# The clearing of an edge layer's sums moved behind its first gathers, on one Trainium2 core

## The reference

```python
def _gine_layer(x, src, dst, edge_attr, eps, We, be, W1, b1, gamma, beta, W2, b2):
    e = edge_attr @ We + be
    m = jax.nn.relu(x[src] + e)
    agg = jax.ops.segment_sum(m, dst, num_segments=x.shape[0])
    h = ((1.0 + eps) * x + agg) @ W1 + b1
    mu = jnp.mean(h, axis=0)
    var = jnp.mean(jnp.square(h - mu), axis=0)
    h = (h - mu) * jax.lax.rsqrt(var + BN_EPS) * gamma + beta
    h = jax.nn.relu(h)
    return jax.nn.relu(h @ W2 + b2)
```

## Time and profile before

| | |
|---|---|
| median of 3 runs | 876.57 us (871.54 to 879.27) |
| the profiled execution | 878.66 us |
| its span, first to last instruction | 876.9 us |
| mean granted clock of PE | 0.965 of full speed |
| busy: PE, DVE, ACT, POOL | 90%, 80%, 62%, 32% of the span |
| an edge layer, from its first gather to its last sum | about 68 us, of which there are four |

### The profile page before, as it was taken

How to read it: one execution, slowest core, us unless ns; L and a number is a source line. 1 busy time by engine, 2 the same in 40 slices (tenths; PEclk the granted TensorE clock), 3 DMA queues, 4 the chain that set the end, 5 groups by cost and what they waited for, 6 DMA issues and landing times.

```text
span 876.9 us, 12030 instructions
## 1 busy us (share of the span) xinstructions
PE 786.6 (90%) x3566; PEld 601.8 (69%) x3566; DVE 697.3 (80%) x1253; ACT 543.0 (62%) x1034; POOL 283.1 (32%) x230
## 2 busy tenths in 40 slices
PE   2979899899889899979999999988999989999895
PEld 2667565477467668756777777776777867878674
DVE  7989856799966968886798878977889778997635
ACT  2288213566563423556797778877788677864656
POOL 3000387877300000016760067400863028610000
PEclk9989999799989999997999999999999999999998
DMA  5323246788472330417994199823996249942001
GB/s 117 103 80 107 69 131 195 227 248 243 150 261 85 118 131 1 154 39 178 215 223 120 35 222 222 206 92 84 225 221 161 86 126 215 220 105 65 32 6 54
DMA packets 61329, 122.12 MB, mean 139 GB/s; under 512 B 9096, under 2 KB 22698, under 8 KB 61269
## 3 DMA queue, kind: packets, MB, share of 16 engines
q0 software_dynamic: 22096, 52.18, 27.2%
q1 hardware_dynamic: 39173, 69.17, 25.1%
HBM read 105.60 MB, written 15.73 MB: 138 GB/s over the span
## 4 chain that ended last, share of the span: by engine, by line
PE 59%; DVE 21%; ACT 11%; DMA 6%; issue 3%; SPq 0%; ACTq 0%; DVEq 0%
PE ps L712 12%; PE ps L1043 9%; PE ps L1082 6%; PE ps L1026 6%; PE ps L1067 6%; DVE z_parts L1955 5%; PE ps L820 5%; DMA onehot_dst<-onehot_rows 4%; PE ps L965 3%; PE ps L911 3%; DVE gathered_parts L1702 2%; DVE w L1462 2%; PE ps L704 2%; ACT slot_recs L1146 2%; ACT queued L1298 2%
## 5 line engine op out<-in xcount | busy, mean ns | idle before, releaser
L680 POOL DMA_INDIRECT queued<-node_rows,srci x92 | 144.4, 1569 | 198.3 <-DMA node_rows<-work 152.1
L1043 PE MATMUL ps<-z_parts,onehot_dst 128*125 128x512 f32 x664 | 189.4, 397 | 2.9 <-DMA onehot_dst<-onehot_rows 2.6
L1955 DVE SCALAR_TENSOR_TENSOR z_parts<-ps,z_parts 128x512 fp32r<-128x512 f32 x216 | 146.0, 689 | 34.5 <-ACT z_parts L1354 30.0
L712 PE MATMUL ps<-w,xT 128*125 128x512 f32 x660 | 169.2, 409 | 3.7 <-DVE w L1462 2.7
L1354 ACT ACTIVATE z_parts<-ps 128x512 fp32r<-128x512 f32 x216 | 128.1, 598 | 49.8 <-PE ps L1026 44.6
L712 PEld LDWEIGHTS ps<-w,xT 128*125 128x125 f32 x660 | 125.0, 193 | 35.1 <-issue 5.7
L1043 PEld LDWEIGHTS ps<-z_parts,onehot_dst 128*125 128x125 f32 x664 | 121.0, 186 | 39.9 <-issue 11.5
L1026 PE MATMUL ps<-x_parts,gather_lhs 128*128 x408 | 130.5, 401 | 5.1 <-DVE z_parts L1955 5.1
L1026 PEld LDWEIGHTS ps<-x_parts,gather_lhs 128*128 128x128 f32 x408 | 76.9, 189 | 26.0 <-issue 8.0
L674 POOL DMA_INDIRECT gathered<-rel_rows,rowi x75 | 77.8, 1037 | 22.8 <-issue 22.2
L1955 DVE SCALAR_TENSOR_TENSOR z_parts<-queued,z_parts 128x512 fp32r<-128x512 f32 x116 | 79.5, 685 | 5.8 <-ACT z_parts L1354 5.6
(11 more groups left out here) (285 smaller groups left out, 1125.8 us busy)
## 6 DMA issues: line engine op xcount, KB each, us to landing
w_stage<-in_weights SPq DMA_DIRECT2D x88, 256.0 KB, 3.8
onehot_dst<-onehot_rows SPq DMA_DIRECT2D x80, 250.0 KB, 5.1
onehot_rows<-onehot_dst SPq DMA_DIRECT2D x20, 250.0 KB, 2.4
gather_lhs<-edge_src_rows SPq DMA_DIRECT2D x8, 432.0 KB, 7.9
node_rows<-work SPq DMA_DIRECT2D x20, 160.0 KB, 2.0
queued<-node_rows,srci POOLq DMA_INDIRECT x116, 6.5
node_rows<-work SPq DMA_DIRECT2D x20, 90.0 KB, 2.0
rel_rows<-rel_rows_out SPq DMA_DIRECT2D x10, 160.0 KB, 1.9
```

The lines of the kernel that those rows point to most:

```text
L680: gp.indirect_dma_start(Q[k % QR][:, :], None, xb_d, row, compute_op=ALU.add)\
L712: mm = pe.matmul(ps[0:R, bank, :], lt[:, a, k, n * R:(n + 1) * R], w[:, b, k, :], start=first and k == 0 and (a, b) == THREE[0], stop=last ...
L1043: mm = pe.matmul(psf[0:R, bass.ds(d, D)], S[:, j // SK % SR, j % SK, :], Z[:, g % ZR, a, :], start=False, stop=False, skip_group_check=True)
L1955: v.scalar_tensor_tensor(out=Z[:, g % ZR, LO, :], in0=of, scalar=0.0, in1=Z[:, g % ZR, HI, :].bitcast(F32), op0=ALU.max, op1=ALU.subtract) ...
```

## The change

On PE, `zeros(0)` to `zeros(3)` stand ahead of the loop, right behind the gathers of tiles 0 to 2, and each waits for the copy of its own row tile alone. `zeros(4)` stays where all five were, and waits for the fifth copy. On ACT the copy of the fifth row tile is made in the next layer, behind the high part of its second message tile.

```diff
@@ PE @@
+                for b in range(NT - 1):
+                    if l:
+                        pe.wait_ge(x_kept, NT * (l - 1) + b + 1)
+                    zeros(b)
                 for i in range(TE + LAG):
...
                     if i == LAG - 1:
                         if l:
                             pe.wait_ge(x_kept, NT * l)
-                        for b in range(NT):
-                            zeros(b)
+                        zeros(NT - 1)
@@ ACT @@
+            def keep(l, n):
+                act.wait_ge(xb_made, NT * (l + 1) + n + 1)
+                nc.scalar.activation(X[0:R, n, :], ps[0:R, n, :], ACT.Relu).then_inc(x_kept, 1)
+
             for l in range(NL2):
...
                     nc.scalar.activation(Z[:, g % ZR, HI, :], of, ACT.Relu).then_inc(z_hi, 1)
+                    if l and i == 1:
+                        keep(l - 1, NT - 1)
...
-                    for n in range(NT + 1):
-                        if n < NT:
-                            act.wait_ge(w2_done, NT * l + n + 1)
-                            nc.scalar.activation(XS[0:R, HI, n, :], ps[0:R, n, :], ACT.Relu).then_inc(xs_hi, 1)
+                    for n in range(NT):
+                        act.wait_ge(w2_done, NT * l + n + 1)
+                        nc.scalar.activation(XS[0:R, HI, n, :], ps[0:R, n, :], ACT.Relu).then_inc(xs_hi, 1)
                         if n:
-                            act.wait_ge(xb_made, NT * (l + 1) + n)
-                            nc.scalar.activation(X[0:R, n - 1, :], ps[0:R, n - 1, :], ACT.Relu).then_inc(x_kept, 1)
+                            keep(l, n - 1)
```

## The result

The changed kernel took 872.97 us in the median (869.7 to 884.47, 12 runs), the kernel before 876.86 us (871.54 to 879.71, 12 runs) on the same chip: a ratio of 0.9953, 95% interval 0.9933 to 0.9974. That is 0.5% or some 4 us faster, where 872.0 us was forecast. (The ratios in this document leave out runs that lie more than 1.5% above the fastest of their kernel, here the one of 884.47 us, so they need not be those of the medians.) The profiled execution took 873.43 us with a span of 871.7, against 878.66 and 876.9.

The account below looks back on a forecast made before the run. PE was taken to bound the kernel (busy 90% of the span, 59% of the chain). Layers 1 to 3 at 0.48 + 0.87 = 1.35 us each, 4.05, plus 0.5 in layer 0, made 4.5: median 872.0 us, range 866 to 878.5.

Parts of the forecast that it names:

- The copy: Start of layers 1 to 3: without the fifth copy ahead, ACT's first high part comes earlier, gaining 0.48 us each.
- The copy shows: Rival, layers 1 to 3: tile 2's high part or the fifth zero late beyond cover; gain 3.0, 873.5 us; chance 0.10.
- The zeros: Start of layers 1 to 3: four zeros fill PE's idle time ahead of tile 3's gather, gaining 0.87 us each.
- forecast spare time of 0.30 us: Layers 1 to 3: four zeros issued by 716.41, ahead of tile 3's gather at 716.71.
- Layer 0: Its start has no copy and runs at half clock; zeros partly hidden, gain 0.5 us.
- the clock rises sooner: Rival, layer 0: filling PE's pause of 0.64 us brings full clock up to 3.9 us earlier; gain 6.4, 870.1; chance 0.07.
- The lead is passed on: From start to end of each layer: DVE fills up earlier by the same 1.35 us, so the lead lasts.
- The transfers keep the old time: Rival, layers 1 to 3: earlier one-hot loads meet the same backlog, land as before; gain about 1 us, 875.6; chance 0.18.
- The transfers get worse: Rival, all four layers: earlier one-hot loads meet more of POOL's DMAs and take longer; 882 us; chance 0.05.
- the first rest tile of layer 1: POOL's first indirect DMA stays put while ACT takes its tile earlier: slack of 2.0 us becomes 0.65, still covered.
- the waits for one-hot loads: Sign in the changed profile: PE's waits for one-hot loads still near 0.7 us in a layer.

Follow-up runs that it names:

- after_again: The changed kernel, unaltered, measured and traced a second time: 875.9 us, ratio 0.9985 to the kernel before.
- copy_only: Kernel before with only the fifth copy moved behind the second message tile, all five zeros left behind the gather of tile 3: 875.8 us, ratio 0.9987.
- before_again: The kernel before, unaltered, run once more for a second trace: 886.94 us.
- no_loads_before: Kernel before without the one-hot loads behind the first three groups of each edge layer, those groups being reused: 869.79 us, ratio 0.9941 to the kernel before.
- no_loads_after: Changed kernel without the one-hot loads behind each edge layer's first three groups: 903.45 us on another chip, ratio 0.9865 to the kernel before (913.98 us there).
- after_third: The changed kernel, unaltered, a third time, on the chip where the kernel before took 913.98 us: 912.15 us, ratio 0.9956.
- five_ahead: Against the kernel before, all five zeros ahead of the gather of tile 3, the fifth copy in its old place: 872.79 us, one run; kernel before 875.93.
- zeros_twice: Changed kernel with four more products with zeros ahead of the gather of tile 3: 877.27 us, one run, where the kernel before took 875.93.

## Why the prediction was right, and where it was not

**The time** came within 1 us of the forecast (872.97 against 872.0), partly by luck: the median of such runs moves by more than that (875.9 for the changed kernel in after_again, 878.52 for the kernel before beside it). The changed kernel's three ratios are 0.9953, 0.9985 and 0.9956; only the second has 1 in its interval. A gain of 3.1 to 3.5 us in layers 1 to 3 and 0.2 to 0.6 in layer 0 would be 0.4 to 0.5%, and all three agree with it. The traces thus show a gain of 3.3 to 4.1 us where the sum had 4.5.

**The copy: right.** 0.48 us forecast, 0.45 measured, alone (copy_only) and in the change. ACT's high part and DVE's low part moved as the step said. *The copy shows* fell: behind the fifth zero PE goes straight on to the gathers, and DVE's 0.18 us of waiting ahead of the low part of tile 2 holds nobody up.

**The zeros: right mechanism, mis-sized term.** The step took four zeros out of the stretch at their full price, 0.87 us. Measured were 0.66 with the old copy and, in the change, 0.60 (1.05 less 0.45). The step said that 0.87 us "leaves the stretch in which PE is needed", and counted only the array's work. Between the gather of tile 3 and the first sums PE's sequencer spends 0.66 us on two loads of offsets, and the zeros that left were its cover. With the loads moved, the start reaches 4.45 us, 1.33 less than before: the 1.35 of the prediction to 0.02. The forecast spare time of 0.30 us behind the four zeros was right (0.31).

The page "Advanced Engine Details and Errata" of the Trainium skill (Sequencer Loop) says that a sequencer pushes engine instructions into a queue and starts control instructions itself. By that these loads would cost nothing as long as the array has queued work. The traces agree: none of their 0.66 us shows in the kernel before, 0.22 to 0.27 with one zero as cover. The page also says that other engine instructions can be queued while a control instruction runs; no row here shows that.

**Layer 0: the forecast of 0.5 us holds only like with like.** In the two first traces the start fell by 2.4 us, near *the clock rises sooner*. But the kernel before has an early rise too (before_again 6.19 us, no_loads_before 6.15), and with an early rise the changed one took 5.57 to 5.95 (after, after_again): 0.2 to 0.6 us less. The nearest pair is the one without the loads, with the rise 3.4 us behind the first product in both: 6.15 and 5.61, 0.54 less, which is the 0.5 forecast (no_loads_after: gather of tile 5 at 438.16, first gather product at 432.55). With a late rise it was 7.99 and 8.02 (before, copy_only) against 6.87 in after_third; of that 1.1 us, the clock's rise at 6.1 and not 7.4 us accounts for about half of 1.3, an estimate, which leaves some 0.5 again.

Behind the first product the rise came after 7.4, 7.5, 3.6 and 3.4 us in four traces with the pause, and after 3.0 to 4.2 in eight of nine without it and 6.1 in the ninth. So filling the pause does not ensure an early rise. Whether it makes one more likely is open: two were late of four, and one of nine.

In the first pair the rest of layer 0 took 64.36 us against 63.51. The loads do not explain that: PE waited 0.7 us for them there, and 1.0 us in the kernel before. What the changed kernel's trace has more is two waits for low parts of DVE. Waits of PE in layer 0, before and after:

```profile
PE ps L1043 <- DMA onehot_dst<-onehot_rows: 1.0, 2, 0.6
```

```profile
PE ps L1046 <- DVE z_parts L1962: 1.2, 2, 0.7
PE ps L1046 <- DMA onehot_dst<-onehot_rows: 0.7, 1, 0.7
```

copy_only, with the start of the kernel before, has 1.1 us of such waits for DVE too, and after_third none. So the 0.85 us are not shown to come of the change.

By the page "TensorE: Matmul & The Clock Gate" of the Trainium skill (Part 1: The HAM clock gate) the full clock follows sustained activity. after_third, busy throughout and late, shows that unbroken work alone did not fix the moment; no run here shows what did.

**The lead is passed on: right.** *The transfers keep the old time* would have let the rests grow by what the starts gained. Without the loads in question they did not grow at all, and with them the changed kernels' rests, 250.2 to 251.7, lie about those of the kernel before, 250.49 and 252.18. *The transfers get worse* fell with it: in the changed kernel the one-hot loads of layer 3 land 5.6 us behind their issue in the median, before 6.0.

```profile
DMA to landing us min/median/max: 4.7/5.6/6.3
```

And the first rest tile of layer 1, forecast to have 0.65 us left:

```profile
DMA to landing us min/median/max: 6.3/6.8/7.7
```

```profile
506.00 1.54 POOL L680 DMA_INDIRECT queued<-node_rows,srci  x1 [50.66 <-DMA node_rows<-work]
...
514.46 0.63 ACT L1361 ACTIVATE z_parts<-queued 128x512 fp32r<-128x512 f32 x1
```

Even at 7.7 us it has landed by 513.7, and ACT takes the tile at 514.46: 0.76 us are left, with 2.0 before.

What did not hold among the signs: the waits for one-hot loads do not stay near 0.7 us. In layers 1 to 3 together PE waits 1.7 and 2.3 us for them in the two traces of the kernel before, and 0, 1.3 and 0 in the three of the changed kernel. Layer 3 of before_again alone has two such waits, 1.1 us in all.

The loads as a whole cost some 4 to 5 us of the kernel (ratio 0.9941, and rests of 246.8 for 250.5 to 252.2), which is as much as the change gained.

## What to carry to other kernels

Before moving cheap instructions of an engine into its idle time, look at what that engine's sequencer does at the place that they leave: register loads and the like are free only under work that the engine already has queued, so move them along. When an edit is worth a few tenths of a microsecond, read it off from one product to another inside its stretch, which repeated here to 0.04 us (but for layer 2's 0.15), and not off the time, which scatters by 1 to 2%. To see whether a lead lasts, take a suspected source of scatter out of both kernels and compare what is left.

## What the runs showed of the hardware that was not expected

- Two TENSOR_LOAD of PE's sequencer, 0.33 us each, cost nothing with five queued products of 0.22 us, 0.22 to 0.27 us with one and, worked out from five_ahead, 0.45 us with none. In zeros_twice, 0.55 us more of array work ahead cost only 0.22 us, since the loads then ran under it.
- With the same instructions in the same order, the granted clock at the start of layer 0 rose 3.6 or 7.4 us behind the first product in two traces of the kernel before, and the window of 23 us ahead of the edge layers ran at 0.50 or 0.78. In the ten traces off the slower chip, whose programs do not differ ahead of edge layer 0, the clock in this window goes with where edge layer 0 begins: at 0.50 to 0.55 the first gather product stands at 402.3 to 405.4, at 0.62 and 0.63 at 398.8 and 398.1, and at 0.76 to 0.78 at 394.2 to 396.4. So most of the scatter of these runs arises ahead of the edge layers.
- The slower chip granted less clock early on. The windows below, of the changed kernel on two chips, show 0.95 and 0.82 for the same 161 us from the start of the span, with 639 and 475 products. The span of after_third is 41.3 us longer (913.0 and 871.7), all of it ahead of edge layer 0 (first gather product at 437.31 against 395.35); why was not looked into.

```profile
129.00:290.00 161.00, 145.12 (x639) 102.76 (x638) 128.01 (x236) 86.72 (x150) 75.98 (x74) 0.95 0.67 207
```

```profile
129.00:290.00 161.00, 117.31 (x475) 78.51 (x476) 103.97 (x188) 67.34 (x118) 76.26 (x74) 0.82 0.52 153
```
